# A four-layer graph network on one core: two instead of three buffers for the high parts, seven instead of six pairs in the adjacency ring

## The chip, the cores and the metric

The kernel runs on one core of a Trainium2 chip. The metric is the device time of one execution in microseconds; the median of several runs is given.

## What is computed

`x` is 8192 x 64, `adj` is 8192 x 8192 (one entry in 512 is not zero, and the diagonal). Four layers, each added to its input and normalised over the 64 features:

```python
# layer 0
h = jnp.tanh(jnp.concatenate([X, tcol], axis=1) @ W1 + b1)
XB = X @ B.T
return h @ W2 + b2 + adj @ XB - jnp.sum(adj, axis=1, keepdims=True) * XB
# layer 1: Chebyshev terms, three products with adj one after the other
T_curr = adj @ x
T_next = 2.0 * (adj @ T_curr) - T_prev          # twice
# layer 2
h_neigh = (adj @ X + X) / deg
out = relu(concat([X, h_neigh]) @ W + b), rows divided by their length
# layer 3: only the last 100 non-zero entries of a row count
rank = jnp.cumsum(adj != 0, axis=1)
w = mask * jnp.where(pos > 0, 0.5 ** (k - pos), 0.0)
out = w @ (x @ weight) + bias
```

Layers 0 to 2 need five products of `adj` with 64 (or 128) columns. Layer 3 needs the ranks of the non-zero entries.

## The kernel before

The adjacency is cut into 8 x 8 blocks of 1024 x 1024, and each block into four chunks of 1 MB ("pairs": two slices of 128 source rows by 1024 target columns). Every pair is brought from HBM by one transfer of SyncE into a slot of the ring `raw` (`NR` = 6 slots of 8 KB per partition, L382). The matrix does not stay on the chip: it is streamed for each sweep over it again.

There are five sweeps for layers 0 to 2 (`k` = 1 to 5, 832 pairs) and a last pass for layer 3 (256 pairs). Sweep 1 takes all 64 blocks (256 pairs), the others 36 blocks (144 pairs each), since the products of two layers' steps are put into one sweep: `sweep_groups` (L15) cuts a sweep into groups of blocks per block row `r`: "D" is one diagonal block, "P" and "S" are `r` and `8 - r` blocks. Each group adds up in one of two PSUM accumulators `ACC`.

Products are made in two parts for precision. For each pair c

- ScalarE (`split_hi`, L423 to L428) rounds `raw` to the high part `hi`, a ring of `NH` = 3 buffers of 8 KB per partition. It waits for the transfer, for `hi_used` (TensorE has finished the high matmuls of pair c - NH) and for `lo_done` (VectorE has subtracted pair c - NH);
- VectorE (`split_lo`, L595 to L597) subtracts: `lo = raw - hi`, in place of `raw`;
- TensorE (`multiply`, L837 to L865) does eight matmuls with `hi` (four where only one part of the operand counts: D groups and sweep 5; L857), then four with `lo` (L864), then raises `pair_done`. SyncE waits for `pair_done` of pair c - NR before it fills the slot again (L376 to L378).

Between the pairs stand the steps of the layers at the end of each block row. Each engine's program is one list: for pair c the split or the multiply, then the steps that are due at c (`due`, L197 to L310). So a step stands behind the engine's own work for pair c, and everything for pair c + 1 stands behind the step. For a block row that ends with pair c in sweep 1: TensorE does `comb` after pair c + 3 (many small matmuls, L906 to L923), VectorE `fin_a` after c + 6 (L651 and the following, up to the variance, L628), ScalarE `root` after c + 9 (the square root, L440), VectorE `fin_b` after c + 8 (it waits for the root; L636 to L645), TensorE `tp` after c + 10, `w02` after c + 13. In sweeps 2 to 4 `comb` is due at c + 2 and `fin_a` at c + 5 (its first instruction is L644 in sweep 2), in sweep 4 `root` at c + 8 and `fin_b` at c + 7. In sweep 5 `comb` is at c + 2, `fin_a` (L671) at c + 5, followed by a longer chain for relu, length and normalisation that goes to and fro between ScalarE and VectorE; two pairs before the row's end TensorE transposes (`tpx`, L869) for it.

In the last pass no high part is made: VectorE counts the non-zero entries out of `raw` (`count`, L612), TensorE turns counts into ranks (`rank`, L966) and weighs (`weigh`, L980), ScalarE makes the weights (L434).

Of the kernel before, what the change touches and what calls it, by code (L numbers as in the profile page):

```python
# [36 lines left out]
def graph_layers(nc, at, x_rows, x_cols, t_col, b_t, w1, w1_t, b1_c, w2, bias_rows, l1_w, l2_w, l3_w,  # L37
# [10 lines left out]
    G = N // P  # L48
    Q = BLK // P
    NP = 4  # L50
    NR = 6
    NH = 3
    NW = 4
    HALF = 512
    HID = w1.shape[1]
# [10 lines left out]
    def place(name, shape, dt, at_byte=None):  # L66
        size = 2 if dt == bf16 else 4
        for n in shape[1:]:
            size *= n
        off = (at_off[0] + 31) // 32 * 32 if at_byte is None else at_byte  # L70
        if at_byte is None:
            at_off[0] = off + size
        return nc.alloc_sbuf_tensor_at(name, shape, dt, offset=off), off
# [5 lines left out]

    raw, raw_at = place("raw", [P, NR, 2, BLK], f32)  # L80
    lo, _ = place("lo", [P, NR, 2, BLK], f32r, raw_at)
    hi, _ = place("hi", [P, NH, 2, BLK], f32r)
    UT, UT_at = place("UT", [P, BLK], f32)
# [44 lines left out]

    raw_in = [sem(f"raw_in{s}") for s in range(NR)]
    hi_done, lo_done = sem("hi_done"), sem("lo_done")  # L130
# [232 lines left out]
    with nc.Block() as block:  # L363

        @block.sync
        def _(sp):
            for c in range(n_all):
# [5 lines left out]
                else:  # L373
                    I, o = divmod(c - n_pairs, NB * NP)
                    J, pr = divmod(NB * NP - 1 - o, NP)
                s, before = c % NR, c - NR  # L376
                if 0 <= before < n_pairs:
# [41 lines left out]
        def _(act):  # L419
# [3 lines left out]
            def split_hi(c):  # L423
                act.wait_ge(raw_in[c % NR], 16 * (c // NR + 1))
                if c >= NH:
                    act.wait_ge(hi_used, c - NH + 1)
                    act.wait_ge(lo_done, c - NH + 1)
                nc.scalar.copy(hi[:, c % NH], raw[:, c % NR]).then_inc(hi_done, 1)  # L428

# [108 lines left out]
        def _(dve):  # L538
# [55 lines left out]
            def split_lo(c):  # L594
                p = pairs[c]  # L595
                dve.wait_ge(hi_done, c + 1)
                tt(lo[:, c % NR], raw[:, c % NR], hi[:, c % NH].bitcast(f32), ALU.subtract).then_inc(lo_done, 1)  # L597

# [454 lines left out]
def build(nc, arrays, N, D):  # L1053
    args = [nc.dram_tensor(f"in_{n}", arrays[n].shape, mybir.dt.float32, kind="ExternalInput").ap() for n in _INS]
    out = nc.dram_tensor("out_0", (N // 1024, 128, 8, D), mybir.dt.float32, kind="ExternalOutput").ap()
    graph_layers(nc, *args, out)
# [13 lines left out]
```

## Time and profile before

| | |
|---|---|
| three runs, median | 3195.03 us (3191.19 to 3198.87) |
| the profiled execution | 3194.05 us, its span 3192.2 us |
| TensorE (matmuls), busy | 3066.3 us, 96% |
| VectorE, busy | 2833.2 us, 89% |
| ScalarE, busy | 2346.9 us, 74% |
| read from HBM | 1145.77 MB, 360 GB/s over the span |
| chain that ended last | TensorE 75%, VectorE 18%, DMA 3%, issue 2%, ScalarE 2% |

The chain of work that ended last is followed back from the last instruction, at each step to what released it. Matmuls overlap each other at their ends, so a TensorE that is busy all the time is one that never waits, not one at its peak. TensorE's work differs from stretch to stretch, and so does the engine that it waits for; sweep 1 ends at about 850 us, sweep 4 at about 2051 us, sweep 5 at about 2465 us.

### The profile page before, as it was taken

To read this page: it belongs to the slowest core of one execution; us is meant where nothing else is said; L and a number is where in the kernel's file an instruction comes from. 1 tells how busy PE (TensorE), PEld (TensorE's weight loads), DVE (VectorE), ACT (ScalarE), POOL (GpSimd) and SP (SyncE) were. 2 spreads that over 40 slices of the span, in tenths; PEclk is the share of its full clock that TensorE was granted. 3 is DMA by queue.
4 is the path that set the end of the run, shared out by engine and by line. 5 is a ranking of instruction groups with operands and counts; after the bars stand their busy time and mean duration, and the time that the engine had idled before them with its cause. 6 is when DMAs were issued, how large, how long until landed. Compare 5 with 4: busy or idle time off the path is not lost.

```text
span 3192.2 us, 36363 instructions
## 1 busy us (share of the span) xinstructions
PE 3066.3 (96%) x14003; PEld 2284.6 (72%) x14066; DVE 2833.2 (89%) x2403; ACT 2346.9 (74%) x1598; POOL 21.0 (1%) x46
## 2 busy tenths in 40 slices
PE   7999999999999999899998999988988999999998
PEld 5887888788868888688876788767766555555554
DVE  7878787778799888998889989899999999999997
ACT  5666666666677767876677776787777788888887
POOL 2000000000000000000000000000000000000000
PEclk9999999999999999999999999999999999999999
DMA  9888788888899999999999999998999999999996
GB/s 345 343 335 318 296 329 321 319 314 334 310 369 394 382 368 386 384 398 379 370 385 366 378 384 368 387 354 332 364 388 398 375 384 383 383 378 384 389 384 256
DMA packets 159450, 1150.26 MB, mean 360 GB/s; under 512 B 18016, under 2 KB 18208, under 8 KB 19952
## 3 DMA queue, kind: packets, MB, share of 16 engines
q1 hardware_dynamic: 157824, 1143.02, 91.8%
q0 software_dynamic: 1168, 4.53, 0.5%
q8 instruction: 113, 1.85, 0.2%
q14 instruction: 57, 0.47, 0.0%
q10 hardware_dynamic: 288, 0.39, 0.0%
HBM read 1145.77 MB, written 2.10 MB: 360 GB/s over the span
## 4 chain that ended last, share of the span: by engine, by line
PE 75%; DVE 18%; DMA 3%; issue 2%; ACT 2%; SPq 0%; ACTq 0%; DVEq 0%
PE ACC L857 32%; PE ACC L864 17%; PE ACC L966 13%; DVE lo L597 13%; PE PST L980 4%; PE PSF L980 3%; DMA raw<-in_at 3%; ACT hi L428 1%; PE PST L869 1%; PE PSF L923 1%; PE PST L895 1%; DVE SV L709 1%; PE PSF L921 1%; DVE M L612 1%; PE PSF L946 1%
## 5 line engine op out<-in xcount | busy, mean ns | idle before, releaser
L428 ACT CAST hi<-raw 128x2048 fp32r<-128x2048 f32 x832 | 1589.9, 1916 | 655.4 <-PE ACC L857 505.2
L597 DVE TENSOR_TENSOR lo<-raw,hi 128x2048 fp32r<-128x2048 f32 x832 | 1880.9, 2288 | 207.4 <-ACT hi L428 204.0
L857 PE MATMUL ACC<-hi,T 128*128 128x512 f32 x5568 | 1415.1, 393 | 10.9 <-ACT hi L428 9.3
L857 PEld LDWEIGHTS ACC<-hi,T 128*128 128x128 f32 x5568 | 1046.2, 189 | 246.0 <-issue 16.9
L864 PE MATMUL ACC<-lo,T 128*128 128x512 f32 x3200 | 875.6, 396 | 84.3 <-DVE lo L597 81.7
L864 PEld LDWEIGHTS ACC<-lo,T 128*128 128x128 f32 x3200 | 595.6, 189 | 249.2 <-DVE lo L597 129.2
L612 DVE SCALAR_TENSOR_TENSOR M<-raw,M 128x512 bf16<-128x512 f32 x1008 | 636.9, 686 | 41.0 <-PE ACC L966 24.2
L434 ACT ACTIVATE Wf<-ACC,w_bias 128x1024 fp32r<-128x1024 f32 x512 | 569.6, 1116 | 127.1 <-PE ACC L966 126.5
L966 PE MATMUL ACC<-M,rank_b 128*128 128x512 bf16 x1969 | 518.4, 382 | 12.3 <-ACT Wf L434 6.7
L966 PEld LDWEIGHTS ACC<-M,rank_b 128*128 128x128 bf16 x2032 | 158.9, 98 | 266.6 <-issue 131.7
L980 PE MATMUL PST<-Wf,S 128*128 128x512 f32 x512 | 209.0, 489 | 0.0
L980 PE MATMUL PSF<-Wf,S 128*128 128x512 f32 x512 | 208.0, 487 | 0.3 <-ACT Wf L434 0.3
L980 PEld LDWEIGHTS PST<-Wf,S 128*128 128x128 f32 x512 | 97.6, 191 | 37.2 <-issue 0.6
L980 PEld LDWEIGHTS PSF<-Wf,S 128*128 128x128 f32 x512 | 97.2, 190 | 37.3 <-ACT Wf L434 0.7
L923 PE MATMUL PSF<-w_sb,hT 128*128 128x64 f32 x256 | 47.0, 316 | 0.0
L864 PE MATMUL ACC<-lo,ST 128*128 128x512 f32 x128 | 36.1, 404 | 9.0 <-DVE lo L597 8.3
L923 PEld LDWEIGHTS PSF<-w_sb,hT 128*128 128x128 f32 x256 | 41.6, 231 | 0.0
L651 DVE COPY RS<-PSF 128x8 f32<-128x8 f32 x8 | 1.3, 166 | 40.1 <-PE PSF L923 40.1
L864 PEld LDWEIGHTS ACC<-lo,ST 128*128 128x128 f32 x128 | 22.9, 188 | 19.4 <-DVE lo L597 15.4
L479 ACT COPY SV<-ACC 64x1024 f32<-64x1024 f32 x28 | 28.3, 1011 | 11.5 <-PE PSF L926 5.0
L716 DVE TENSOR_TENSOR SV<-SV,ACC 64x1024 f32<-64x1024 f32 (+1 forms) x28 | 34.1, 1217 | 1.2 <-PE ACC L864 0.8
L857 PE MATMUL ACC<-hi,ST 128*128 128x512 f32 x128 | 34.8, 394 | 0.0
(150 smaller groups left out, 1033.7 us busy)
## 6 DMA issues: line engine op xcount, KB each, us to landing
raw<-in_at SPq DMA_DIRECT2D x1088, 1024.0 KB, 6.2
O<-in_x_rows SPq DMA_DIRECT2D x8, 256.0 KB, 7.2
SV<-in_x_cols POOLq DMA_DIRECT2D x1, 2048.0 KB, 17.5
out<-O POOLq DMA_DIRECT2D x7, 256.0 KB, 6.3
out<-O ACTq DMA_DIRECT2D x1, 256.0 KB, 2.0
bias<-in_bias_rows ACTq DMA_DIRECT2D x1, 128.0 KB, 3.8
l1w_sb<-in_l_w POOLq DMA_DIRECT2D x2, 64.0 KB, 7.4
rank_f<-in_rank_mats POOLq DMA_DIRECT2D x1, 128.0 KB, 8.7
```

The costliest lines, as they stand in the source:

```text
L428: nc.scalar.copy(hi[:, c % NH], raw[:, c % NR]).then_inc(hi_done, 1)
L434: nc.scalar.activation(Wf[:, m % NW, :], rank_banks[m % 2], ACT.Exp, scale=-LN2, bias=w_bias[:, 0:1]).then_inc(wt_done, 1)
L597: tt(lo[:, c % NR], raw[:, c % NR], hi[:, c % NH].bitcast(f32), ALU.subtract).then_inc(lo_done, 1)
L612: ins = stt(M[:, (m + 1) % Q, part], src, 0.0, M[:, m % Q, part], ALU.not_equal, ALU.add)
L709: tt(SV[u, cols(I)], SV[u, cols(I)], ACC[acc_of[k, "D", r]][u, :], ALU.add).then_inc(sv_dve, 1)
L716: tt(SV[part, cols(I)], SV[part, cols(I)], ACC[acc_of[k, "P", r]][part, :], ALU.add).then_inc(sv_dve, 1)
L857: ins = mm(acc[:, part], w, hi[:, p.c % NH, s, part], start=p.opens and s == 0 and i == 0, stop=False)
L864: ins = mm(acc[:, part], ws[s][0], lo[:, p.c % NR, s, part], start=False, stop=p.closes and s == 1)
L869: last = mm(dst[0:D, q * P:(q + 1) * P], src[:, q, :], eye[:], start=True, stop=True)
L923: last = mm(PSF[:, q, 0:D], hT[:, c, part], w2_sb[:, c, :], start=False, stop=c == HC - 1)
L966: ins = mm(rank_banks[m % 2][:, part], rank_b[:, mat, :], M[:, slot, part], start=i < 2, stop=i >= len(terms) - 2)
L980: ins = mm(out_acc[I % 2][:, part], S[:, g, :], Wf[:, m % NW, part], start=o == 0, stop=o == G - 1)
```

## The change

The ring `raw` gets a seventh slot, the ring `hi` loses one of its three buffers. Both are 8 KB per partition, so everything behind them in memory stays where it is. All waits follow from the two numbers: pair c's transfer waits for pair c - 7 to be multiplied, and pair c's high part for pair c - 2 to be used by TensorE and subtracted by VectorE. The instructions and their order on each engine are the same.

```diff
     Q = BLK // P
     NP = 4
-    NR = 6
-    NH = 3
+    NR = 7
+    NH = 2
     NW = 4
     HALF = 512
```

## Rows read from the trace of the kernel before

**Rows 1.** The page's groups: line, form, xcount | busy us, mean ns | idle before, releasers.

```profile
L428 ACT CAST hi<-raw 128x2048 fp32r<-128x2048 f32 x832 | 1589.9, 1916 | 655.4 <-PE ACC L857 505.2 <-DMA raw<-in_at 103.7 <-DVE lo L597 34.1
L597 DVE TENSOR_TENSOR lo<-raw,hi 128x2048 fp32r<-128x2048 f32 x832 | 1880.9, 2288 | 207.4 <-ACT hi L428 204.0
```

**Rows 2.** Stretches: us, busy (count) of PE, PEld, DVE, ACT, POOL, PEclk, DMA share, GB/s.

```profile
100.00:848.00 748.00, 748.00 (x3489) 608.48 (x3489) 589.83 (x366) 494.11 (x288) 0.00 (x0) 0.99 0.84 323
848.00:2051.00 1203.00, 1166.35 (x5261) 953.46 (x5260) 1103.61 (x622) 886.05 (x511) 0.00 (x0) 0.99 0.97 377
2051.00:2465.00 414.00, 367.84 (x1766) 287.28 (x1765) 396.61 (x276) 319.87 (x227) 0.00 (x0) 0.97 0.94 367
2465.00:3192.00 727.00, 707.53 (x3194) 376.71 (x3256) 669.65 (x1075) 592.77 (x546) 3.83 (x7) 0.99 0.94 369
```

**Rows 3.** Instructions in order of time, a steady pair of sweep 1: start, us, engine.

```profile
425.00 1.98 PE L857 MATMUL ACC<-hi,T 128*128 128x512 f32 x8
...
427.05 1.92 ACT L428 CAST hi<-raw 128x2048 fp32r<-128x2048 f32 x1 [0.80 <-PE ACC L857]
...
429.01 2.29 DVE L597 TENSOR_TENSOR lo<-raw,hi 128x2048 fp32r<-128x2048 f32 x1 [0.43 <-ACT hi L428]
...
434.97 1.07 PE L864 MATMUL ACC<-lo,T 128*128 128x512 f32 x4
```

**Rows 4.** In order of time, TensorE behind `comb`, sweep 1, row that ends at 127.

```profile
451.44 2.09 PE L857 MATMUL ACC<-hi,T 128*128 128x512 f32 x8
...
461.54 1.07 PE L864 MATMUL ACC<-lo,T 128*128 128x512 f32 x4
...
466.98 1.12 PE L864 MATMUL ACC<-lo,T 128*128 128x512 f32 x4
```

**Rows 5.** In order of time, VectorE and ScalarE at the same row end.

```profile
445.31 2.29 DVE L597 TENSOR_TENSOR lo<-raw,hi 128x2048 fp32r<-128x2048 f32 x1 [0.41 <-ACT hi L428]
451.66 0.17 DVE L651 COPY RS<-PSF 128x8 f32<-128x8 f32 x1 [4.06 <-PE PSF L923]
...
457.01 4.48 DVE L597 TENSOR_TENSOR lo<-raw,hi 128x2048 fp32r<-128x2048 f32 x2
...
461.00 1.28 ACT L440 ACT_TABLE_LOAD   x1
462.29 0.21 ACT L440 ACTIVATE st<-st 128x8 f32<-128x8 f32 x1
...
462.53 0.20 DVE L636 RECIPROCAL st<-st 128x8 f32<-128x8 f32 x1 [1.04 <-ACT st L440]
...
464.56 6.69 DVE L597 TENSOR_TENSOR lo<-raw,hi 128x2048 fp32r<-128x2048 f32 x3
```

**Rows 6.** In order of time, a row end of sweep 2 (pair 347).

```profile
1123.18 2.07 PE L857 MATMUL ACC<-hi,T 128*128 128x512 f32 x8
...
1125.09 0.69 DVE L644 CAST T<-PSF 128x512 fp32r<-128x512 f32 x1
...
1133.26 1.07 PE L864 MATMUL ACC<-lo,T 128*128 128x512 f32 x4
```

**Rows 7.** In order of time, a row end of sweep 5 (pair 779).

```profile
2325.40 1.56 PE L857 MATMUL ACC<-hi,T 128*128 128x512 f32 x4
...
2336.67 1.18 PE L857 MATMUL ACC<-hi,T 128*128 128x512 f32 x4
...
2338.94 0.69 DVE L671 TENSOR_TENSOR sq<-PSF,RD 128x512 f32<-128x512 f32 x1
```

**Rows 8.** Stretches over two `comb` steps of sweep 1, columns as in rows 2.

```profile
335.30:350.40 15.10, 15.10 (x78) 13.94 (x77) 7.72 (x9) 1.91 (x1) 0.00 (x0) 0.66 0.34 132
443.30:453.50 10.20, 10.20 (x77) 9.36 (x77) 5.63 (x6) 1.91 (x1) 0.00 (x0) 1.00 0.48 195
```

**Rows 9.** In order of time, a late transfer in sweep 2.

```profile
1012.19 1.92 ACT L428 CAST hi<-raw 128x2048 fp32r<-128x2048 f32 x1 [2.80 <-DMA raw<-in_at]
...
1020.73 1.20 PE L864 MATMUL ACC<-lo,T 128*128 128x512 f32 x4 [0.61 <-DVE lo L597]
```

## The prediction

> **What bounds the kernel now.** I read the groups of the page first, for the three engines that hand a pair of chunks on: ScalarE's rounding to the high part (L428) takes 1.92 us, VectorE's subtraction (L597) 2.29 us [rows 1]. Then the table by stretch [rows 2]: TensorE is busy for 748.00 of 748 us in sweep 1, for 1166 of 1203 in sweeps 2 to 4, for 368 of 414 in sweep 5 and for 708 of 727 in the ranked last layer. VectorE has 590 of 748 us in sweep 1 and 397 of 414 in sweep 5. So TensorE sets the time of sweep 1 without a gap, VectorE nearly sets sweep 5, and sweeps 2 to 4 change between the two. ScalarE is never the bound by its work. Its idle time before L428 is 655 us, of which 505 ended when TensorE had used a high part, and 104 when a transfer landed [rows 1]. A wait for a buffer that costs nothing is what one wants to see there: ScalarE runs as far ahead as its three buffers let it.
>
> How far that is, one pair in steady state shows [rows 3]. TensorE's eight high matmuls end at 425.00 + 1.98 = 426.98; ScalarE starts the pair three further on at 427.05, VectorE subtracts from 429.01 to 431.30, and TensorE comes to that low part at 434.97. From "high part used" to "new low part ready" are 4.32 us, and the low part is there 3.67 us before it is wanted. A pair takes TensorE 2.72 us there (two of them from 461.54 to 466.98, [rows 4]).
>
> **What the change does.** No instruction is added, taken away or moved on any engine; only what two waits wait for changes. ScalarE's high part of pair c waits for pair c - 2 to be used by TensorE and subtracted by VectorE, no longer for pair c - 3. The transfer of pair c waits for pair c - 7, no longer for c - 6. In the steady state the first costs the lead one pair: 3.67 - 2.72 = 0.95 us are left. That is still above zero, so the steady stretches keep their pace. The cost arises where a step on VectorE or ScalarE is longer than 0.95 us, and where the order of the steps counted on three.
>
> **Sweep 1, the largest term.** At the end of a block row TensorE does `comb` after pair c + 3, and VectorE does `fin_a` after its own pair c + 6. With three buffers the high part of c + 6 needs TensorE's c + 3, which stands before `comb`; with two it needs c + 4, which stands behind it. Take the row that ends at pair 127. Now VectorE has subtracted pair 133 (445.31 to 447.60), waits 4.06 us for `comb`, and starts `fin_a` at 451.66, which holds it until 457.01 [rows 5]. With two buffers pair 133 is rounded only when TensorE has used pair 131, the first behind `comb`: 451.44 + 2.09 = 453.53 [rows 4]. Plus 4.32, `fin_a` starts at 457.85, 6.2 us later. It takes the same 5.35 us, to 463.2; pair 134's subtraction ends at 465.5, and TensorE wants it at 461.54 [rows 4]: 3.9 us of stall. Then the square root: ScalarE takes it behind the high part of pair 136, which now waits for VectorE's pair 134 (465.5). 465.5 + 1.92 + 1.28 for the table + 0.21 gives 468.9, where the reciprocal (L636) starts at 462.53 now [rows 5]. From it to the next subtraction are 2.03 us, so pair 136 is subtracted at 471.0 + 2.29 = 473.3, wanted at 466.98 [rows 4], where it is 0.13 us early now. Together TensorE is 6.3 us late; what the second stall adds lies on top of the first, and both come from the one shift of 6.2. TensorE has no gap in this sweep to take it back [rows 2]. Eight row ends have this order: 8 x 6.2 = 50 us. What else waits: the transposes and `w02` behind `fin_b` just move along.
>
> **Sweeps 2 to 4.** Here `comb` stands after c + 2 and `fin_a` after VectorE's c + 5, so the same thing happens, with shorter steps. In rows that are followed by another P group, TensorE has pace 2.72: behind `comb` the high matmuls end at 1123.18 + 2.07 = 1125.25, `fin_a` (L644) would start at 1129.57 in place of 1125.09, 4.5 us later; 3.67 us of lead are there to pay it [rows 3, 6]. 0.8 us are left over, visible at the pair wanted at 1133.26. Sweep 4 has a square root too; less the table of 1.28 us its share is 2.2 - 1.28 = 0.9 more. Three such rows per sweep: 3 x (0.8 + 0.8 + 1.7) = 10 us. The other five rows of each sweep are followed by D blocks, with eight matmuls per pair in place of twelve, where VectorE is often late already, so the lead that can be lost is not always there. I bound one by 0.8 below (as above) and 2.7 above (a whole pair) and take 1.5, nearer to the first since much of the lead is spent before: 15 x 1.5 = 22 us, ends 12 and 41.
>
> **Sweep 5.** Behind `comb` the high matmuls end at 2336.67 + 1.18 = 2337.85; plus 4.32, `fin_a` (L671) starts at 2342.2 in place of 2338.94: 3.2 us later [rows 7]. VectorE has hardly any idle time here (17 of 414 us, [rows 2]), so this stays. There is a second place in each row: the transposes `tpx` hold TensorE until 2325.40, its first high matmuls behind them end at 2326.96 [rows 7], and what VectorE could work ahead meanwhile is one pair (2.3 us) less. Between 2.6 (3.2 less 0.6 of the lead there) and the 6.2 of sweep 1 I take 4.4 for each of seven rows: 31 us, ends 18 and 43.
>
> **The clock.** In one of the `comb` stretches the granted clock is 0.66 in the mean, which is a stay at 1.2 GHz, in another 1.00; the same 77 or so matmuls take 15.1 and 10.2 us [rows 8]. What TensorE did before it fell is many short matmuls without a pause. Sweep 1 now gets stalls of 4 us close to these. That costs nothing if the clock does not mind, and 8 x 4.9 = 39 us if it falls in every row. I take two more falls, 10 us.
>
> **The seventh pair.** It could take away ScalarE's waits for transfers, 103.7 us in all [rows 1]. Where one shows, 2.80 us of it became 0.61 us on TensorE [rows 9]; and the later start of the high parts covers most of these waits from now on. That leaves 0 to 5 us; I take 2 off. The last layer uses no high part, TensorE is busy for 97% of it [rows 2], and a deeper ring does not feed it faster: 0.
>
> **Sum.** 50 + 10 + 22 + 31 + 10 - 2 = 121 us on the profiled execution's 3194.05 us gives 3315; its own time is 1 us below the median of 3195.03, so the prediction is 3316.
>
> **Rivals.** *Only the exact places pay.* If the stalls of the D blocks and of sweep 5 fall into waits that are there anyway and no clock falls, 50 + 10 remain: 3255. For it speaks that VectorE is late there already; against it that a late VectorE is on the path, and its shift is then the path's.
>
> *The cascade.* Every end at its top: 50 + 10 + 41 + 43 + 39 = 183, 3378. The clock is what would do it.
>
> *Two buffers are enough.* TensorE needs 2.72 us for a pair, ScalarE 1.92 and VectorE 2.29, and 0.95 us of lead stay. If steps that run ahead find their buffer free after all, nothing changes: 3195. Against it stands the order: pair c + 6 is behind `comb` by the wait itself. The Trainium skill (Trainium Kernel Development and Optimization, Best Practices) gives "Double-buffer for performance" as its rule, which names two and would make this rival right; the row with the 4.06 us wait speaks against it, since there the buffers carry not one engine's overlap but the distance between steps of three.
>
> *The ring was the bound.* This one ends faster. The mechanism: a transfer that could not start because its slot was held, ScalarE waiting for it, VectorE and TensorE behind. It decides if these waits reach TensorE and the high buffers do not bind there. By the ratio 0.61 to 2.80 all 103.7 us are worth 23 us: 3171; if each reached TensorE whole, 3090. The SBUF page of the Trainium skill (SBUF — State Buffer) holds HBM to be "almost always your end-to-end bottleneck"; by it this rival would be the likely one. The trace has DMA busy at 0.97 in sweeps 2 to 4, but at 0.84 in sweep 1, with TensorE full [rows 2].
>
> **Chances.** Forecast (from 3194 + 50 + 10 + 12 + 18 - 5 = 3279 up to 3372) 0.68; only the exact places (about 3255) 0.12; cascade 0.08; two are enough 0.06; ring 0.06. The range goes from 3250 to 3372: at the bottom it takes in the first rival, at the top it stops short of the cascade; 0.2 lies outside. A measurement of this kernel can tell 0.2%, some 6 us, from no change. Slower 0.88, within 0.06, faster 0.06.
>
> **What would show it.** In the profile after: L651's wait for `comb` (4.06 us in the row read) gone, and in its place VectorE's wait for ScalarE before it; TensorE with waits for the low part in sweep 1, of about 4 and 2 us in each row end, and the stretch of sweep 1 longer by some 50 us; steady pairs still at 2.72 us with the low part about 1 us early; sweep 5 longer by about 30 us; the last layer unchanged at 727 us; ScalarE's waits for transfers well under 104 us. The forecast is wrong if sweep 1 keeps its length (then the order argument fails), or if sweep 1 grows as said and sweeps 2 to 5 shorten (then transfers had been the bound there).

## The result and the profile after

The changed kernel takes 3368.69 us (median of 4 runs, 3356.73 to 3370.11), the kernel before in the same comparison 3196.28 us. The ratio is 1.0543, with a 95% interval from 1.0524 to 1.0563: 5.4% slower, 172 us where 121 were forecast. The profiled execution took 3370.11 us, its span is 3368.3 us, 176.1 us more than the span before.

Three groups of the page of the changed kernel (columns as in [rows 1]), and its line on the chain of work that ended last:

```profile
PE 70%; DVE 20%; ACT 6%; issue 2%; DMA 1%; ACTq 0%; SPq 0%; DVEq 0%
...
L597 DVE TENSOR_TENSOR lo<-raw,hi 128x2048 fp32r<-128x2048 f32 x832 | 1889.7, 2289 | 411.3 <-ACT hi L428 408.3
L428 ACT CAST hi<-raw 128x2048 fp32r<-128x2048 f32 x832 | 1587.6, 1912 | 887.1 <-PE ACC L857 665.4
...
L864 PE MATMUL ACC<-lo,T 128*128 128x512 f32 x3200 | 897.2, 403 | 174.0 <-DVE lo L597 171.8
```

Both works are as long as before (1.91 and 2.29 us each); only the idle time ahead of them is longer. ScalarE waited 665 us for TensorE (505 in [rows 1]), VectorE 408 us for ScalarE (204 in [rows 1]). The view of waits over the whole changed kernel (who waited for what: us in total, times, longest) tells the rest:

```profile
DVE lo L597 <- ACT hi L428: 408.3, 463, 13.3
...
PE ACC L864 <- DVE lo L597: 182.9, 152, 9.5
ACT hi L428 <- DVE lo L597: 180.0, 140, 6.2
...
ACT hi L428 <- DMA raw<-in_at: 24.6, 8, 11.5
```

The two lines of the same view of the kernel before that this changes most:

```profile
PE ACC L864 <- DVE lo L597: 90.1, 69, 10.6
...
DVE RS L651 <- PE PSF L923: 40.1, 8, 7.2
```

The waits for transfers are nearly gone, 24.6 us against 103.7 [rows 1]. TensorE's waits for low parts doubled. And VectorE's eight waits for `comb` (40.1 us), one of which is the 4.06 us of [rows 5], are in no line any more: `fin_a` is reached after `comb` has ended.

Where the time went, by sweeps. The cuts are the moments at which TensorE finished the last pair of a sweep (columns as in [rows 2]). First the changed kernel, then the kernel before at its own cuts:

```profile
100.00:905.90 805.90, 776.01 (x3513) 625.34 (x3512) 595.35 (x368) 496.39 (x291) 0.00 (x0) 0.96 0.79 302
905.90:1339.00 433.10, 408.12 (x1809) 330.78 (x1809) 366.65 (x198) 293.60 (x170) 0.00 (x0) 0.97 0.91 349
1339.00:1749.30 410.30, 389.19 (x1730) 312.65 (x1729) 365.72 (x206) 297.05 (x168) 0.00 (x0) 1.00 0.96 369
1749.30:2170.90 421.60, 391.70 (x1729) 312.01 (x1729) 375.74 (x220) 292.95 (x175) 0.00 (x0) 1.00 0.94 359
2170.90:2641.40 470.50, 389.97 (x1745) 294.68 (x1745) 397.54 (x276) 315.75 (x225) 0.00 (x0) 0.93 0.86 320
2641.40:3368.00 726.60, 707.24 (x3186) 375.98 (x3246) 668.49 (x1072) 591.60 (x545) 3.84 (x7) 0.99 0.93 366
```

```profile
100.00:853.50 753.50, 753.50 (x3513) 613.04 (x3513) 595.28 (x368) 498.80 (x291) 0.00 (x0) 0.99 0.84 324
853.50:1261.30 407.80, 398.74 (x1810) 327.62 (x1809) 365.81 (x198) 294.75 (x170) 0.00 (x0) 0.98 0.95 371
1261.30:1655.90 394.60, 383.47 (x1729) 312.89 (x1728) 364.74 (x206) 297.30 (x168) 0.00 (x0) 1.00 0.98 383
1655.90:2057.70 401.80, 385.33 (x1729) 313.96 (x1729) 373.46 (x220) 294.13 (x175) 0.00 (x0) 1.00 0.97 377
2057.70:2467.00 409.30, 363.14 (x1744) 283.14 (x1744) 392.04 (x275) 315.56 (x224) 0.00 (x0) 0.97 0.94 367
2467.00:3192.00 725.00, 705.53 (x3186) 375.27 (x3246) 668.37 (x1072) 592.26 (x545) 3.83 (x7) 0.99 0.94 369
```

By the first number behind the cut: sweep 1 is 52.4 us longer, sweep 2 25.3, sweep 3 15.7, sweep 4 19.8, sweep 5 61.2, the last pass 1.6. TensorE, full throughout sweep 1 before, is idle for 29.9 us of it now. In sweep 5 VectorE is idle for 73.0 us (470.5 - 397.54) in place of 17.3, which is 55.7 of the 61.2 us.

**A steady pair** of the changed kernel's sweep 1, the four instructions of [rows 3] in the same order:

```profile
431.37 1.98 PE L857 MATMUL ACC<-hi,T 128*128 128x512 f32 x8
...
433.42 1.91 ACT L428 CAST hi<-raw 128x2048 fp32r<-128x2048 f32 x1 [0.80 <-PE ACC L857]
...
435.37 2.29 DVE L597 TENSOR_TENSOR lo<-raw,hi 128x2048 fp32r<-128x2048 f32 x1 [0.42 <-ACT hi L428]
...
438.62 1.07 PE L864 MATMUL ACC<-lo,T 128*128 128x512 f32 x4
```

The low part is ready at 435.37 + 2.29 = 437.66 and wanted at 438.62: a lead of 0.96 us (0.95 forecast), and two pairs from 433.18 to 438.62 still take 2.72 us each.

**The row that ends at pair 127**, the changed kernel, which [rows 4, 5] show before. VectorE:

```profile
480.15 2.29 DVE L597 TENSOR_TENSOR lo<-raw,hi 128x2048 fp32r<-128x2048 f32 x1 [12.58 <-ACT hi L428]
482.36 0.16 DVE L651 COPY RS<-PSF 128x8 f32<-128x8 f32 x1
...
487.70 4.49 DVE L597 TENSOR_TENSOR lo<-raw,hi 128x2048 fp32r<-128x2048 f32 x2
493.55 0.20 DVE L636 RECIPROCAL st<-st 128x8 f32<-128x8 f32 x1 [1.36 <-ACT st L440]
```

TensorE and ScalarE in the same stretch:

```profile
484.52 1.98 PE L857 MATMUL ACC<-hi,T 128*128 128x512 f32 x8
490.04 2.07 PE L864 MATMUL ACC<-lo,T 128*128 128x512 f32 x4 [3.54 <-DVE lo L597]
491.91 3.62 PE L857 MATMUL ACC<-hi,T 128*128 128x512 f32 x8
```

```profile
490.09 1.90 ACT L428 CAST hi<-raw 128x2048 fp32r<-128x2048 f32 x1 [4.31 <-DVE lo L597]
492.01 1.28 ACT L440 ACT_TABLE_LOAD   x1
```

This is the chain that was worked out. Ahead of `fin_a` VectorE now waits 12.58 us for the high part and none for `comb`. TensorE stalls 3.54 us (3.9 forecast), and ScalarE waits for VectorE before the square root's pair. The matmuls behind the stall took 2.07 and 3.62 us in place of 1.07 and 1.98; this was not foreseen (last section).

### The profile page after: what moved, and what is told of

It reads as the page before. It is cut to its first block, busy times and chain, and to the rows that moved or that the text cites. A ratio compares the mean times of both kernels' runs of the same rounds, so it can differ in the third digit from the quotient of the medians.

```text
span 3368.3 us, 36363 instructions
## 1 busy us (share of the span) xinstructions
PE 3139.3 (93%) x14003; PEld 2309.6 (69%) x14066; DVE 2841.3 (84%) x2403; ACT 2339.4 (69%) x1598; POOL 20.9 (1%) x46
## 4 chain that ended last, share of the span: by engine, by line
PE 70%; DVE 20%; ACT 6%; issue 2%; DMA 1%; ACTq 0%; SPq 0%; DVEq 0%
PE ACC L857 28%; PE ACC L864 15%; DVE lo L597 13%; PE ACC L966 12%; ACT hi L428 5%; PE PST L980 3%; PE PSF L980 3%; PE PST L869 1%; PE PSF L923 1%; DMA raw<-in_at 1%; PE PSF L926 1%; PE PSF L946 1%; PE PST L895 1%; DVE M L612 1%; PE PSF L930 1%
## 5 line engine op out<-in xcount | busy, mean ns | idle before, releaser
L857 PE MATMUL ACC<-hi,T 128*128 128x512 f32 x5568 | 1436.6, 398 | 18.5 <-ACT hi L428 9.4
L857 PEld LDWEIGHTS ACC<-hi,T 128*128 128x128 f32 x5568 | 1058.5, 192 | 264.1 <-issue 25.8
L864 PE MATMUL ACC<-lo,T 128*128 128x512 f32 x3200 | 897.2, 403 | 174.0 <-DVE lo L597 171.8
L926 PEld LDWEIGHTS PSF<-comb,SV 128*128 128x128 f32 x256 | 30.8, 194 | 7.0 <-issue 6.2
L926 PE MATMUL PSF<-comb,SV 128*128 128x128 f32 x256 | 32.6, 281 | 2.7 <-DVE O L752 2.3
```

The source lines that it names most:

```text
L857: ins = mm(acc[:, part], w, hi[:, p.c % NH, s, part], start=p.opens and s == 0 and i == 0, stop=False)
L864: ins = mm(acc[:, part], ws[s][0], lo[:, p.c % NR, s, part], start=False, stop=p.closes and s == 1)
L926: last = mm(PSF[:, q, :], SV[:, qs[q]], (comb2, comb3)[k - 2][:], start=True, stop=True)
```

## The experiments

All ratios are to the kernel before, run beside each kernel on the same chip; the sweeps' times are read from one profiled execution of each.

**Was it the high buffers or the ring?** The first two each change one number of the new pair.

`e1_two_high_six_slots`, against the changed kernel:

```diff
-    NR = 7
+    NR = 6
     NH = 2
```

> The kernel before with two high buffers alone, six slots kept (8 KB per partition left unused). Theory (the high buffers do it all, the seventh slot is worth nothing): as the changed kernel, 3369 us within 8 us, since in its trace a landed pair lies 5 to 9 us before ScalarE takes it. Rival (the seventh slot gives something back that the high buffers cost): 3385 us or more.

Measured: 3362.62 us, ratio 1.0532 (1.0515 to 1.0549), where the change itself has 1.0543 (1.0524 to 1.0563). The intervals overlap: with two high buffers the seventh slot is worth nothing that can be measured. The loss is the third high buffer's. (A seventh slot with three high buffers was not tried.)

`e2_three_high_five_slots`:

```diff
-    NR = 7
-    NH = 2
+    NR = 5
+    NH = 3
```

> Three high buffers, one ring slot fewer than before. Asks what a slot is worth where the high buffers do not bind. If the ring is no bound even at six: 3196 us within 8 us. Mine: in sweeps 2 to 5 a pair lands 0 to 2.5 us before ScalarE takes it, and would come 2.7 us later, which the lead of 3.7 us covers in long P groups and not in D blocks and sweep 5: 3230 to 3290 us.

Measured: 3249.38 us, 1.0178 (1.0163 to 1.0193). Here a slot counts: from six to five costs 1.8%. In the view of waits of this kernel ScalarE's longest line is the one for transfers:

```profile
ACT hi L428 <- DMA raw<-in_at: 562.7, 620, 11.9
```

`e6_four_high_five_slots` makes the trade the other way round:

```diff
-    NR = 7
-    NH = 2
+    NR = 5
+    NH = 4
```

> The trade made the other way: five slots in the ring, four high buffers. Three high buffers with five slots took 3249 us, sweeps 2 to 5 each 7 to 30 us longer or unchanged against the kernel before by waits for transfers. If the fourth high buffer gives nothing where TensorE is full and the five slots bind: 3249, within 10. If ScalarE running four ahead makes up for transfers that come late: 3195 to 3225. If it takes the slots in use up sooner and no more: 3249 to 3265.

Measured: 3248.84 us, 1.017 (1.0145 to 1.0195), the same as with three high buffers and five slots. ScalarE's waits for TensorE fall to 47.1 us and those for transfers rise (the view of waits, this kernel):

```profile
ACT hi L428 <- DMA raw<-in_at: 651.8, 658, 12.3
...
ACT hi L428 <- PE ACC L857: 47.1, 14, 9.8
```

With five slots a fourth high buffer buys nothing. Three and six are the best of the pairs tried.

**Is it the order of the steps in sweep 1?** `e3_sweep1_steps_earlier` keeps two high buffers and moves sweep 1's steps one pair forward, so that `fin_a` again stands behind a high part that doesn't wait for TensorE's work behind `comb`:

```diff
-            due("DVE", c + 6, "fin_a", k, r)
-            due("ACT", c + 9, "root", k, r)
-            due("DVE", c + 8, "fin_b", k, r)
+            due("DVE", c + 5, "fin_a", k, r)
+            due("ACT", c + 8, "root", k, r)
+            due("DVE", c + 7, "fin_b", k, r)
```

> The changed kernel (seven slots, two high buffers) with three steps of sweep 1 one pair earlier on their engines: fin_a behind c + 5, root behind c + 8, fin_b behind c + 7. Theory (the order counted on three buffers): fin_a's pair no longer needs a pair behind comb, so VectorE waits for comb again and starts at once behind it. By hand, at the row that ends at 127, stalls of about 0.5 and 2.5 us remain of 6.3: 3.2 us back in each of eight rows, 3343 us within 10 us, sweep 1 some 26 us shorter, other sweeps as they are. Rival (the lead is merely shorter, or the clock costs the time): less than 10 us back.

Measured: 3352.46 us, 1.0492 (1.0474 to 1.0511), 16 us back in place of 26. Sweep 1 ends 13.1 us earlier than with the change, sweep 2 takes 4.9 us less (428.2 for 433.1: the row that ends at 255 has its costs there), the others are within 0.5 us. The first three row ends cost 3.08, 3.05 and 3.07 us in place of 6.4, as worked out (3.1); the next four 4.24 to 4.32. In the first three TensorE's stall is 2.11 to 2.15 us and its clock stays up; in the next four it is 2.47 to 2.48 us and the clock falls. TensorE's low matmuls at the row that ends at 127 show it:

```profile
477.44 1.82 PE L864 MATMUL ACC<-lo,T 128*128 128x512 f32 x4 [2.48 <-DVE lo L597]
```

They run at less than full speed behind the stall (1.07 us is usual). `comb` also met the lower clock in more rows than before the change, 9.7 us in all, against 4.8 us with the change. So the order of the steps is shown to cost about half of a row end; the clock took some 10 us of this back (4.9 us in `comb`, 1.2 us in each of four rows).

`e4_all_steps_earlier` keeps these moves and makes them in sweeps 2 to 5 too: VectorE's steps from `fin_a` to `fin_b` (in sweep 5 to `fin_c`) and ScalarE's `root`, `relu`, `square`, and `keep` in sweeps 2 to 4, one pair forward. The last row of sweep 5 stays as it was. A part of the edit:

```diff
-            due("DVE", c + 5, "fin_a", k, r)
+            due("DVE", c + 4, "fin_a", k, r)
...
-            due("ACT", c + 8, "relu", k, r)
-            due("DVE", c + 7, "length", k, r)
+            due("ACT", c + 7, "relu", k, r)
+            due("DVE", c + 6, "length", k, r)
```

> As the kernel before this one, and in sweeps 2 to 5 too fin_a and the steps up to fin_b (in sweep 5 up to fin_c, but not in its last row) one pair earlier. Theory: the rows followed by P groups lose their 0.8 to 2.1 us altogether (10 us), D blocks about 10 us, sweep 5 about 20 us: 3305 us within 20 us. Rival (in sweep 5 the shorter lead behind tpx does it, not the order): sweep 5 stays within 8 us of the 470 us that it takes in the changed kernel, and the total is 3320 us or more.

Measured: 3333.44 us, 1.0447 (1.0415 to 1.0478), outside the 3305 within 20 that were expected. Sweeps 2 and 3 took 422.4 and 403.7 us (433.1 and 410.3 with the change), and their rows followed by P groups cost nothing any more. Sweep 5 went from 470.5 to 463.1 us only, within the rival's 8 us. There the place of `fin_a` and of the steps behind it is not the main cost. Of the change's 172 us, all moves together give 35 back; no order tried with two buffers comes near the kernel before.

**One pair a row.** `x1_one_pair_per_row_end` is the kernel before with the stricter waits for eight pairs alone, each row's end plus 6 in sweep 1:

```diff
+            fin_pairs = {row_end[1, r] + 6 for r in range(NB)}
...
-                    act.wait_ge(hi_used, c - NH + 1)
-                    act.wait_ge(lo_done, c - NH + 1)
+                    act.wait_ge(hi_used, c - (2 if c in fin_pairs else NH) + 1)
+                    act.wait_ge(lo_done, c - (2 if c in fin_pairs else NH) + 1)
```

> The kernel before with its three high buffers and six slots; only eight of the 832 pairs wait as if there were two (the pair that stands before fin_a in sweep 1, row end + 6). Theory (this one wait per row, not a shorter lead everywhere, makes sweep 1's loss): fin_a starts 6.2 us late as with two buffers; by hand a first stall of 3.9 us and, since the root's pair is not held here, a second of 1.2: 5.1 us a row, 41 us in all, 3232 us within 10. Rival (many small losses over 256 pairs): 3191 us within 10.

Measured: 3229.11 us, 1.0115 (1.01 to 1.013). Sweep 1 is 39.9 us longer up to pair 255. That is what seven rows cost, 5.7 us each, where 5.1 were worked out (41 was the sum for eight). The eighth row's stall, 7.4 us at pair 262, falls into sweep 2. It does not show in that sweep's time (407.0 us for 407.7), since `comb` at the same row end ran at the full clock this time, which gave 5.7 us back. So seven single waits make three quarters of the 52.4 us that the changed kernel lost in sweep 1.

**Which of the two waits?** `x2_wait_for_use_only` and `x3_wait_for_subtraction_only` are the kernel before with one of the two made stricter for all pairs:

```diff
# x2
-                    act.wait_ge(hi_used, c - NH + 1)
+                    act.wait_ge(hi_used, c - 2 + 1)
# x3
-                    act.wait_ge(lo_done, c - NH + 1)
+                    act.wait_ge(lo_done, c - 2 + 1)
```

> The kernel before, three buffers and six slots; all high parts wait for TensorE's use of pair c - 2, but only for VectorE's subtraction of pair c - 3. Theory (TensorE's long steps hold the buffers): nearly the whole loss, 3340 to 3365 us. Rival (VectorE's subtraction holds them, above all in sweep 5, where ScalarE's waits for it rose from 12 to 57 us): under 3300 us.

> The other half: wait for VectorE's subtraction of pair c - 2, but for TensorE's use of pair c - 3 only. Theory: 3191 to 3225 us, what is above 3191 in sweep 5. Rival: 3300 us or more.

Measured: x2 3341.09 us, 1.0465 (1.0449 to 1.0481); x3 3205.63 us, 1.004 (1.0026 to 1.0054). The wait for TensorE's use of the high part is what costs: 4.65 of the 5.4%. That for VectorE's subtraction alone costs 0.4%, though the changed kernel has 180 us of ScalarE's waits ended by it. Added up they are 0.4% short of the whole; what is left needs both.

**Sweep 5.** `x4_two_in_sweep5_only` has the stricter waits in sweep 5 alone:

```diff
-                    act.wait_ge(hi_used, c - NH + 1)
-                    act.wait_ge(lo_done, c - NH + 1)
+                    act.wait_ge(hi_used, c - (2 if pairs[c].k == 5 else NH) + 1)
+                    act.wait_ge(lo_done, c - (2 if pairs[c].k == 5 else NH) + 1)
```

> The kernel before, with both waits as of two buffers in sweep 5 alone. Theory (each sweep's loss is its own and starts where the buffers are two): sweeps 1 to 4 as before, sweep 5 at 470 us in place of 409, in all 3252 us within 10. Rival (sweep 5 lost much because the program came late or short of transfers into it): sweep 5 at 440 us or less.

Measured: 3257.67 us, 1.0201 (1.0186 to 1.0216). Sweep 5 takes 472.9 us, 63.6 more than before, and the others are as before: its loss arises in itself and is not carried in from sweep 4.

The last three divide sweep 5's 144 pairs. `two` takes the place of `pairs[c].k == 5` in the edit just shown:

```diff
# x5
+            two = {row_end[5, r] + d for r in range(NB - 1) for d in (1, 5, 17, 21)}
# x6
+            behind = {row_end[5, r] + d for r in range(NB - 1) for d in (1, 5, 17, 21)}
+            two = {c for c in range(n_pairs) if pairs[c].k == 5} - behind
# x7
+            two = {row_end[5, r] + d for r in range(NB - 1) for d in (8, 9, 13, 14)}
```

> The kernel before (three high buffers, six slots), with the stricter waits of two high buffers for 28 pairs of sweep 5 only: those at c + 1, c + 5, c + 17 and c + 21 of the seven rows that end at pair c, whose pair minus two stands directly behind a step of TensorE (transposes, comb, the later transposes, the layer 3 product). With the waits of two in all of sweep 5 that sweep took 472.9 us instead of 409.3. Theory A (every long step of TensorE makes the next high part, and so VectorE's work, start one pair later, and VectorE has no idle time to catch up): these 28 pairs carry nearly all of it, sweep 5 at 409 + 50 = 459 us (454 to 473), the whole about 3192 + 50 = 3242. Theory B (the loss arises in the chain that goes to and fro between ScalarE and VectorE, relu, root and square): 25 to 35 us, the whole about 3222. Sweeps 1 to 4 as before in both.

> The complement of the run with 28 pairs: the kernel before, with the waits of two high buffers for the other 116 pairs of sweep 5. Theory A: little is left, 5 to 15 us, the whole about 3202. Theory B: 30 to 40 us, about 3227. If both halves cost the full 64 us, either place alone starts the same loss, and if the two sum to well under 64, the places need each other.

> The kernel before, with the waits of two high buffers only for the pairs c + 8, c + 9, c + 13 and c + 14 of sweep 5's seven rows, behind which ScalarE does relu, root, square and root for a waiting VectorE. Theory A: 1 us per row, 7 us in all (3 to 12), the whole about 3199. Theory B: 25 to 40 us, about 3225.

Measured: x5 3238.61 us, 1.0147 (1.0128 to 1.0166); x6 3234.51 us, 1.0123 (1.0098 to 1.0149); x7 3207.04 us, 1.004 (1.0022 to 1.0058). Sweep 5 took 455.5, 449.4 and 418.3 us: 46.2, 40.1 and 9.0 more than the 409.3 before (these are profiled executions; x7's median is 13.5 us above that of the kernel before, its runs spread over 3196 to 3215). Sweep 5 of x5 and of x6 by the view of stretches, and VectorE's wait for ScalarE in the same stretch of each:

```profile
2060.10:2515.60 455.50, 381.16 (x1745) 288.10 (x1744) 394.26 (x275) 310.31 (x224) 0.00 (x0) 0.95 0.88 331
...
DVE lo L599 <- ACT hi L430: 49.3, 27, 6.4
```

```profile
2059.40:2508.80 449.40, 378.81 (x1745) 289.92 (x1744) 396.61 (x276) 314.25 (x225) 0.00 (x0) 0.95 0.89 335
...
DVE lo L600 <- ACT hi L431: 32.3, 25, 5.6
```

The chain between ScalarE and VectorE (theory B) is not the cause: its own four pairs a row cost 9 us, 25 to 40 were expected of it. The 28 pairs behind TensorE's steps do cost what theory A said, 46 of 50 us. But the complement costs 40 where theory A said 5 to 15, and the halves sum to 86, more than the whole. (Some 5 of the 40 lie behind the row that ends at 687, in the first pairs of sweep 5, of which x5 holds none.) So theory A is right on the place in the row and wrong on the single pair. In x6, between the pairs' ends, the delay grows by 1.0 us at pair 781 and by 1.0, 0.4 and 1.3 us at 785 to 787, where x5 has 1.0 and 0.9 at 780 and 781 and 1.0, 1.7 and 0.4 at 784 to 786: if the first pair behind the step is let go early, the next one is held instead. That it is one held distance, which any of several pairs sets, fits all four runs; it was inferred from them and not tried by itself.

## Why the prediction was right in kind and short by 50 us

The measured time lies inside the stated range, 3 us under its top of 3372, and that is partly luck. The top was made of every term's high end. Sweep 5 and the row that ends at 255 went beyond what was given for them, while the falls in `comb` took 5 us, net, of the 39 that the clock's high end allowed.

**The mechanism was right.** 4.65 of the 5.4% are the distance of ScalarE's wait for TensorE (x2), in sweep 1 at the row ends (x1), where a step stands between the two pairs. Steady pairs kept their pace with 0.96 us of lead. The last pass moved by 1.6 us.

**Sweep 1's seven rows.** 6.3 us were worked out for a row end ("together TensorE is 6.3 us late") and 6.2 booked; from pair c + 4 to c + 12 each took 6.30 to 6.46 us longer, 45 us in the seven rows to 223.

**The row that ends at 255** was mis-sized. It falls into the first D blocks of sweep 2, and was booked at 6.2 like the others. From the end of pair 255 to that of pair 279 the changed kernel lost 16.9 us: 12.1 up to pair 267, before any step of the next row, and 4.9 behind it, where the steps of that row, which ends at 267, stand too. The longest stall in it is at pair 262 (rows of the changed kernel):

```profile
939.10 4.49 DVE L597 TENSOR_TENSOR lo<-raw,hi 128x2048 fp32r<-128x2048 f32 x2
...
941.44 2.07 PE L864 MATMUL ACC<-lo,T 128*128 128x512 f32 x4 [6.82 <-DVE lo L597]
```

The stall of `fin_a` is 3.9 us after pairs of 2.72 us, because 3.67 us of lead went into it. D pairs take TensorE 1.81 us while VectorE needs 2.29, and there is no such lead: in the kernel before TensorE started on the low parts of pairs 262 to 265 only 0.05 us after each was ready. x1 shows the same 7.4 us at this pair with only pair 261 held.

**Sweeps 2 to 4.** Rows followed by P groups were worked out at 0.8, 0.8 and 1.7 us. They cost 0.7 to 0.8 us in sweep 2, 1.1 in sweep 3, 2.1 in sweep 4: 12 us for 10. (For sweep 4 the sum took 2.2 us as the second stall, where its own rows give 6.3 - 3.9 = 2.4; with that a row comes to 1.9.) Rows followed by D blocks cost 32 us up to the end of sweep 4 (25.3 - 16.9 - 2.3 = 6.1, then 15.7 - 3.3 = 12.4 and 19.8 - 6.3 = 13.5), where 22 were taken between 12 and 41. The row that ends at 687 is not among them: its cost falls into sweep 5.

**Sweep 5 was the step that failed**: 31 us taken, 61 measured, with a stated top of 43. (3.7 of the 61 are lost before the sweep's first row ends, behind row 687, and belong to the D blocks; 57 are left.) What was worked out there was exact. The changed kernel, in order of time, at the row that ends at 779 ([rows 7] before), TensorE:

```profile
2497.24 1.17 PE L857 MATMUL ACC<-hi,T 128*128 128x512 f32 x4
```

and VectorE:

```profile
2487.45 2.29 DVE L597 TENSOR_TENSOR lo<-raw,hi 128x2048 fp32r<-128x2048 f32 x1 [1.89 <-ACT hi L428]
...
2500.44 2.29 DVE L597 TENSOR_TENSOR lo<-raw,hi 128x2048 fp32r<-128x2048 f32 x1 [2.46 <-ACT hi L428]
2502.64 0.68 DVE L671 TENSOR_TENSOR sq<-PSF,RD 128x512 f32<-128x512 f32 x1
...
2509.50 0.69 DVE L733 TENSOR_REDUCE st<-sq 128x8 f32<-128x512 f32 x1 [1.04 <-ACT sq L506]
```

`fin_a` starts 4.23 us after TensorE's high matmuls behind `comb` (2497.24 + 1.17 = 2498.41; forecast 4.32), 1.09 us before: 3.1 later. But two places a row were counted, `tpx` and `comb`. In x4, whose delay can be followed pair by pair, the row that ends at 803 costs 2.1 us at c + 1 to c + 3 (behind `tpx`), 3.1 at c + 5 to c + 7 (behind `comb`), and then 1.0 at c + 8 (relu for a waiting VectorE), 0.5 at c + 13, 1.2 behind `tp` (c + 17, c + 18) and 1.2 behind the layer 3 product (c + 21, c + 22): 9.1 us. The first two make 5.2, inside the 2.6 to 6.2 of the prediction; the other four, 3.9 us, were never in the sum. (At the last pair but one of a row 1.6 us of the delay come back, and the short first rows cost less.) VectorE's waits for the high part in sweep 5, the changed kernel and then the kernel before:

```profile
DVE lo L597 <- ACT hi L428: 49.9, 31, 6.6
```

```profile
DVE lo L597 <- ACT hi L428: 4.9, 7, 1.4
```

That is 45 us of the 61. VectorE was busy for 96% of this sweep, and in the row just followed each of the six places cost time, so there the number of places counts and not only the worst of them. The prediction named that ("hardly any idle time") and then priced the row by its worst end.

**The clock.** Two more falls in `comb`, 10 us, were taken; net there was one more up to pair 255, 4.8 us. The last 2.7 us of sweep 1's 52.4 were in no term: 0.4 to 0.7 us each at pairs 147, 183, 219 and 255, which come four pairs after a P group's end inside a row (the granted clock was 1.00 at all four, so this is not the clock), and the rest in the first 30 pairs. **The seventh pair** was booked at -2 and gave nothing measurable (e1). The low end of that term held.

The Trainium skill calls HBM "almost always your end-to-end bottleneck" (SBUF — State Buffer, section "A bandwidth-pool intuition that's wrong (but worth ruling out)"). This case agrees in part: with two high buffers one slot more bought nothing (e1), while with three high buffers one slot fewer cost 1.8% (e2). The Trainium skill's rule "Double-buffer for performance" (Trainium Kernel Development and Optimization, section "Best Practices") speaks of overlapping DMA with compute. Taken as a number for a buffer that three engines share it is not enough here: e1 is two buffers alone, at 5.3%.

In sum: 45 + 7.5 (sweep 1), 16.9 (row 255), 12 + 32 (sweeps 2 to 4), 61 (sweep 5) and 1.6 make 176 us of span, for 121. Of the 55 between them sweep 5 has 30, row 255 11, the D blocks 10; with the 3.7 us behind row 687 counted as D blocks it is 26 and 14.

## What to carry to other kernels

The number of buffers between engines that run fixed lists is a distance in the order of the steps: before giving one up, list every step of every engine that stands between pair c - 3 and pair c - 2, and ask who is held behind it. Where one engine was full, the worst place of a row gave its price (sweep 1); where an engine was nearly full and lived on working ahead, all places of the row had to be added up (sweep 5). And a wait for transfers that a profile shows says little until one knows that the engine that waits is itself waited for: 79 us of such waits went here, and the kernel became slower.

## What had not been expected of the hardware

**The clock falls behind short stalls, in most cases.** In sweep 1 of the changed kernel each of the seven stalls of 3.5 to 3.8 us is followed by a stay at the lower of the two levels. Three stretches around the stall at the row that ends at 127, before, behind and further behind it (columns as in [rows 2]; the granted clock is the third number from the end):

```profile
478.00:486.00 8.00, 8.00 (x36) 6.59 (x35) 5.68 (x7) 5.74 (x3) 0.00 (x0) 0.98 0.71 259
491.00:495.50 4.50, 4.50 (x12) 3.47 (x11) 3.03 (x5) 2.48 (x3) 0.00 (x0) 0.51 0.50 175
496.50:501.00 4.50, 4.50 (x21) 3.71 (x21) 4.23 (x3) 2.93 (x2) 0.00 (x0) 1.00 0.74 259
```

The middle one is at 1.2 GHz, the last again at 2.4 GHz; what TensorE did before the fall was to wait 3.54 us. The row's end costs 6.30 to 6.46 us nevertheless, nearly what was worked out without this. The likely reason, not tried by itself, is that TensorE's slower matmuls take the place of the second stall of some 2 us, since VectorE's chain sets when the row is over. In x1, where that second stall is shorter, the clock does show in the time. There the row that ends at 63 has a stall of 3.74 us with no fall behind it (granted clock 1.00 from 264.4 to 268.5 us) and costs 4.9 us; the other six rows, with stalls of 3.5 to 3.8 us and a fall behind each, cost 5.6 to 6.5. In sweep 5 of the changed kernel, and of x5 and x6, the clock's mean is lower too (0.93, 0.95 and 0.95 for 0.97); how much of sweep 5's 61 us this is stays open, because VectorE is the bound there and a slower TensorE is partly hidden.

**Whether `comb` meets the lower clock changed from row to row**, with the same instructions: the rows that end at 95, 159 and 255 before, at 31, 127, 223 and 255 after. In sweep 1 it costs 4.8 us each time. Which rows it would be was not to be told from the trace of before; one or two more or fewer of them is 5 to 10 us in any comparison of two such kernels.
